# A transformer block in split float32: attention scores in three runs a batch, and one pool of eight PSUM banks

## The reference

```python
def _attention(xq, xkv, wq, wk, wv, wo, bo):
    q, k, v = (xq @ wq), (xkv @ wk), (xkv @ wv)           # each cut into 16 heads of 64
    attn = softmax(einsum('bihd,bjhd->bhij', q, k) * 64 ** -0.5)
    return einsum('bhij,bjhd->bihd', attn, v).reshape(B, S, 1024) @ wo + bo

h = layernorm(x, ln1);   x = _attention(h, h, sa_...) + x        # self attention
h = layernorm(x, ln2);   x = _attention(h, context, ca_...) + x  # context attention
p = layernorm(x, ln3) @ ff_w1 + ff_b1                            # 256 -> 2048
a, gate = p[..., :1024], p[..., 1024:]
return (a * gelu(gate)) @ ff_w2 + ff_b2 + x
```

## Time and profile before

| | |
|---|---|
| median of 3 runs | 2809.46 us |
| profiled execution | 2807.94 us, of which the span (first to last instruction) is 2806.1 us |
| TensorE matmul (PE) | busy 2785.0 us, 99% of the span, 25278 matmuls |
| PE's weight loads (PEld) | 2491.2 us, 89%, beside the matmuls |
| DVE, ACT, POOL | 79%, 67%, 59% |
| granted TensorE clock | 0.999 of full speed |
| chain that ended last | PE 93%, POOL 3%, DVE 2%, all else 2% or less |
| one self batch, one context batch | 35.88 us, 34.07 us |

### The profile page before, as it was taken

How to read it: one execution, slowest core, us unless ns; L and a number is a source line. 1 busy time by engine, 2 the same in 40 slices (tenths; PEclk the granted TensorE clock), 3 DMA queues, 4 the chain that set the end, 5 groups by cost and what they waited for, 6 DMA issues and landing times.

```text
span 2806.1 us, 73115 instructions
## 1 busy us (share of the span) xinstructions
PE 2785.0 (99%) x25278; PEld 2491.2 (89%) x25278; DVE 2215.6 (79%) x3432; ACT 1885.2 (67%) x5979; POOL 1665.0 (59%) x1500
## 2 busy tenths in 40 slices
PE   8999999999999999999999999999999999999999
PEld 7888888888888888888888888888888899999999
DVE  7888888888888888888888888888888855555554
ACT  6777777777777777877777777777777754444443
POOL 5555555555555555776666666666666655544554
PEclk9999999999999999999999999999999999999999
DMA  6666666666666666677777776777677632222222
GB/s 160 150 162 164 164 161 159 159 153 157 154 149 152 153 155 157 152 183 177 181 177 178 180 177 166 170 172 172 166 169 172 153 100 81 75 78 87 77 75 65
DMA packets 355330, 413.34 MB, mean 147 GB/s; under 512 B 122016, under 2 KB 209440, under 8 KB 355232
## 3 DMA queue, kind: packets, MB, share of 16 engines
q1 hardware_dynamic: 345088, 395.29, 58.1%
q10 hardware_dynamic: 10144, 16.78, 1.6%
HBM read 94.52 MB, written 49.02 MB: 51 GB/s over the span
## 4 chain that ended last, share of the span: by engine, by line
PE 93%; POOL 3%; DVE 2%; DMA 1%; issue 1%; ACT 0%; SPq 0%; DVEq 0%; ACTq 0%; POOLq 0%
PE unit_ps L641 53%; PE unit_ps L666 15%; PE s_ps L653 14%; PE s_ps L641 12%; POOL probs L1375 1%; DVE blocks L1141 1%; DVE neg_max L1127 1%; POOL w_lo L1370 1%; ACT probs L926 0%; DVE qk L1153 0%; DMA pT<-blocks 0%; POOL x_rb L1362 0%; DVE w_lo L1087 0%; DVE hT L1122 0%; DMA out_dram<-x_out 0%
## 5 line engine op out<-in xcount | busy, mean ns | idle before, releaser
L1375 POOL TENSOR_TENSOR probs<-probs,row_inv 128x1024 f32<-128x1024 f32 x512 | 971.9, 1898 | 827.0 <-DVE row_inv L1132 827.0
L926 ACT ACTIVATE probs<-s_ps,neg_max 128x256 f32<-128x256 f32 x2048 | 947.0, 483 | 468.4 <-DVE neg_max L1127 467.4
L1141 DVE STREAM_TRANSPOSE blocks<-probs 128x1024 f32<-128x1024 f32 x512 | 633.3, 1237 | 148.4 <-POOL probs L1375 147.8
L1127 DVE TENSOR_REDUCE neg_max<-s_ps 128x4 f32<-128x1024 f32 x512 | 612.9, 1197 | 12.5 <-PE s_ps L653 5.5
L641 PE MATMUL unit_ps<-hT_hi,w_hi 128*128 128x256 f32 x2048 | 579.9, 287 | 4.2 <-DVE hT_lo L1172 2.3
L641 PE MATMUL unit_ps<-hT_hi,w_lo 128*128 128x256 f32 x2048 | 554.7, 277 | 0.0
L641 PE MATMUL unit_ps<-hT_lo,w_hi 128*128 128x256 f32 x1792 | 497.3, 278 | 0.0
L666 PE MATMUL unit_ps<-pT,v_f 128*64 128x256 f32 x4096 | 456.4, 381 | 0.2 <-DMA pT<-blocks 0.2
L653 PEld LDWEIGHTS s_ps<-qk 64*128 64x128 f32 x6144 | 375.3, 185 | 70.5 <-issue 53.4
L926 ACT ACTIVATION_READ_ACCUMULATOR probs<-s_ps,neg_max 128x1 f32 x2048 | 437.5, 214 | 0.0
L653 PE MATMUL s_ps<-qk 64*128 64x256 f32 x6144 | 427.1, 285 | 5.8 <-ACT probs L926 5.3
(11 more groups left out here) (81 smaller groups left out, 4949.0 us busy)
## 6 DMA issues: line engine op xcount, KB each, us to landing
pT<-blocks SPq DMA_DIRECT2D x1024, 256.0 KB, 4.5
rows_t_dram<-row_blocks SPq DMA_DIRECT2D x91, 256.0 KB, 2.3
rows_in<-rows_t_dram SPq DMA_DIRECT2D x91, 256.0 KB, 4.6
x_res<-in_x_dram SPq DMA_DIRECT2D x32, 256.0 KB, 3.1
x_sa_dram<-x_out SPq DMA_DIRECT2D x32, 256.0 KB, 2.2
x_ln<-x_sa_dram ACTq DMA_DIRECT2D x32, 256.0 KB, 4.5
ctx_in<-in_ctx_dram SPq DMA_DIRECT2D x32, 256.0 KB, 4.1
x_res<-x_sa_dram SPq DMA_DIRECT2D x32, 256.0 KB, 3.4
```

The costliest lines, as they stand in the source:

```text
L926: op = nc.scalar.activation(probs[:, m % 2, r, :].rearrange("p (j b c) -> p j b c", j=IT, c=BLK), scored.rearrange("p (j c b) -> p j b c", ...
L1127: nc.vector.tensor_reduce(neg_max[:, m % RING, :], s_ps[:, m % 2, :, :].rearrange("p h (i j) -> p (h i) j", j=S), AX_X, ALU.max, negate=Tr ...
L1141: nc.vector.transpose(blocks[:, n % 2, :, m % 2, :].rearrange("p b (j r c) -> p r j b c", j=IT, c=BLK), probs[:, m % 2, :, :].rearrange("p ...
L1375: nc.gpsimd.tensor_tensor(probs[:, m % 2, :, :], probs[:, m % 2, :, :], row_inv[:, m % RING, :].unsqueeze(2).broadcast_to([P, ROWS, S]), A ...
```

## The change

**Scores in three runs.** TensorE makes pairs 0, 1, 2, then ("qk", 3 to 7) and the second half of an old projection, then pairs 3, 4, then the four attended units, then pairs 5, 6, 7, then queries and keys 0 to 2 of the next batch, the first half of a projection and the values. In context batches the values come first, and keys and projection alternate. The first batch has five runs, the last three. Loops in self attention run over two batches a round, since the place of the rows alternates.

**One pool.** `s_ps` and `unit_ps` become `ps`, eight banks. A table `DOUBLE_OF` gives each pair's scores one of four double banks, `BANK_OF` each other unit one of eight, and `users_before` finds for every bank of a unit who had it last. The ring of split queries and keys has five places.

**Moved work.** Self attention's rows go to two places in turn, and the lo part goes from DVE to POOL. The last attended unit is split like the others by ACT and DVE (POOL's two instructions and `a_last` go). The values in self attention are all copied by ACT; in context attention DVE copies the third of four. `x_rb` goes: POOL adds the bias in place, and the load of `x_res` now waits until the sum has read it, for which it moves to the start of the next batch. In the feed-forward part the residual moves from position 3 to position 6 in POOL's list.

```diff
-K_BEHIND_Q, QK_APART, QK_RING = 368, 640, 2688
+K_BEHIND_Q, QK_APART, QK_RING = 368, 640, 3328
 RING = 4
+SLOTS = 5
-BANKS = 4
+BANKS = 8
...
-STEP_UNITS = (
-    ((("qk", 3), "cur"), (("qk", 4), "cur"), (("qk", 5), "cur"), (("wo", 1), "old")),
...
+RUNS = ((0, 1, 2), (3, 4), (5, 6, 7))
+DOUBLE_OF = (2, 1, 0, 3, 2, 3, 2, 0)
+SLOT_OF = (0, 1, 2, 3, 4, 0, 1, 2)
...
+END_ORDER = (scored(0, 1, 2) + FIRST_GAP + scored(3, 4) + ATTENDED + scored(5, 6, 7) + VALUES[:2] + OUTPUT_FIRST + VALUES[2:])
...
+BANK_OF = {("qk", 3): 6, ("qk", 4): 7, ("qk", 5): 4, ("qk", 6): 5, ("qk", 7): 2, ("wo", 1): 3, ("x",): 3,
+           ("a", 0): 0, ("a", 1): 1, ("a", 2): 2, ("a", 3): 3,
+           ("qk", 0): 2, ("qk", 1): 3, ("qk", 2): 6, ("wo", 0): 7,
+           ("v", 0, 0): 2, ("v", 0, 1): 3, ("v", 1, 0): 6, ("v", 1, 1): 7}
...
-            with eng.Fori(starting + 1, B - 2, 1) as t:
-                iteration(t, STEADY, sa)
+            with eng.Fori(starting + 1, B - 4, 2) as t:
+                for i in range(2):
+                    iteration(t + i if i else t, STEADY, sa, (starting + 1 + i) % 2)
...
             def scores(t, m, to_context=False):
-                pe.wait_ge(at.qk_lo, g + 1)
-                at_least(pe, at.exp_done, g - 1)
+                at.bank_free(pe, t, ("s", m), "cur", to_context)
...
+                for m in RUNS[0]:
+                    scores(t, m, to_context)
+                for m in range(3, PAIRS):
+                    run_unit(t, home, odd, ("qk", m), "cur")
+                if "old" in parts:
+                    run_unit(t, home, odd, ("wo", 1), "old")
...
+                for m in RUNS[1]:
+                    scores(t, m, to_context)
+                for unit, part in ATTENDED:
+                    run_unit(t, home, odd, unit, part)
+                for m in RUNS[2]:
+                    scores(t, m, to_context)
...
             def residual(ph, b, bias):
                 pool.wait_ge(ph.res_ld, 16 * (b + 1))
-                if ph is not ff:
-                    at_least(pool, ph.wo_done, 2 * b - 1)
-                nc.gpsimd.tensor_tensor(x_rb[:], x_res[:], out_bias[:, bias:bias + 1, :].broadcast_to([P, IT, D]),
+                nc.gpsimd.tensor_tensor(x_res[:], x_res[:], out_bias[:, bias:bias + 1, :].broadcast_to([P, IT, D]),
...
-                    if m == 3 and "cur" in parts:
+                    if m == FT - 2 and "cur" in parts:
                         residual(ff, t, 2)
```

More of the change, by code:

```diff
@@ L23 @@
 FF_WHOLE = 2
-STARTING, TURNING = 6, 4
+STARTING, TURNING = 7, 4
 LOADING, FF_LOADING = 12, 12
@@ L76, in by_tensor, with bank_of, banks_of @@
+BANK_OF = {("qk", 3): 6, ("qk", 4): 7, ("qk", 5): 4, ("qk", 6): 5, ("qk", 7): 2, ("wo", 1): 3, ("x",): 3,
[3 rows of a table added]
+LAST_ATTENDED, LAST_OUTPUT = (4, 5, 6, 4), 5
+ROWS_TURNED, TURNED, DOWN = 1, 6, (4, 7)
+def bank_of(unit, b=None):
+    return 0 if unit == ("qk", 2) and isinstance(b, int) and b == 0 else BANK_OF[unit]
+def banks_of(unit, b):
+    return (2 * DOUBLE_OF[unit[1]], 2 * DOUBLE_OF[unit[1]] + 1) if unit[0] == "s" else (bank_of(unit, b),)
 def by_tensor(b):
     return isinstance(b, int) and b < WHOLE
[L81 to L97, removed]
@@ L100, in units_of, with order_of @@
[L100 to L108, removed]
+def order_of(t, to_context, batches):
+    if isinstance(t, int):
+        special = {-1: FILL_ORDER, 0: START_ORDER, batches - 1: END_ORDER}
+        return special[t] if t in special else SELF_ORDER if t + 1 < batches // 2 else CROSS_ORDER
+    return CROSS_ORDER if to_context else SELF_ORDER
@@ new lines, in users_before @@
+def users_before(t, unit, part, batches, to_context):
+    users = []
+    own = batch_of(t, part)
+    for bank in banks_of(unit, own):
+        at, order = t, order_of(t, to_context, batches)
+        place = order.index((unit, part))
+        while True:
+            place -= 1
+            if place < 0:
+                if isinstance(at, int) and at == -1:
+                    break
+                at = at - 1
+                order = order_of(at, to_context, batches)
+                place = len(order) - 1
+            u, of = order[place]
+            b = batch_of(at, of)
+            if bank not in banks_of(u, b) or (isinstance(b, int) and not 0 <= b < batches):
+                continue
+            if u == ("x",) and not by_tensor(b):
+                continue
+            if not any(u == other for other, _ in users):
+                users.append((u, b))
+            break
+    return users
@@ L668, in attend, with projection @@
                 last.then_inc(at.o_full, 1)
-            def projection(slot, cols, side, tokens):
+            def projection(slot, cols, side, context, tokens):
                 terms = []
@@ L728, in run_unit @@
                     cols = slice(c * HALF * P, (c + 1) * HALF * P)
-                    product(bank, [(h, w) for w, h in projection(2, cols, ph.kv, rows)]).then_inc(at.v_full, 1)
+                    side = 1 if ph.has_ctx else own
+                    product(bank, [(h, w) for w, h in projection(2, cols, side, ph.has_ctx, rows)]).then_inc(at.v_full, 1)
                 elif unit[0] == "wo":
@@ new lines, in attention_iteration @@
+                exponentials(t, 0)
+                split_qk(t, 3)
+                exponentials(t, 1)
+                split_qk(t, 4)
+                if pass_of(t, home).has_ctx:
+                    split_qk(t, 5)
+                    split_qk(t, 6)
+                    exponentials(t, 2)
+                else:
+                    exponentials(t, 2)
+                    split_qk(t, 5)
+                    split_qk(t, 6)
+                split_qk(t, 7)
+                if blocks_next(t, parts):
+                    scale_rows(t + 1, home)
@@ new lines, in attention_iteration @@
+                maxima(t, 4)
+                invert_sums(t, 3)
+                if "old" in parts:
+                    project_out(t - 2, 1)
+                attended_lo(t - 1, 0)
+                invert_sums(t, 4)
+                transpose_blocks(t, 3, home)
+                attended_lo(t - 1, 1)
+                attended_lo(t - 1, 2)
+                if not to_context:
+                    attended_lo(t - 1, 3)
+                maxima(t, 5)
+                if to_context:
+                    attended_lo(t - 1, 3)
@@ new lines, in attention_iteration @@
+                if parts == LAST:
+                    deviation(ff, 0)
+                elif norm_ahead(t, parts):
+                    deviation(at, t + 2)
+                normalise(t, 3)
+                normalise(t, 4)
+                residual(at, t - 1, pass_of(t - 1, home).norm)
+                for p in lo_pool(t, 1):
+                    split_piece(p)
+                normalise(t, 5)
+                if to_context:
+                    context_remainders(t + 1)
+                normalise(t, 6)
```

823 lines of the change are left out of this document (481 added, 342 removed), and 7 rows, old and new, of tables (BANK_OF, STEP_UNITS).

## The result

The changed kernel takes 2908.8 us (median of 4 runs, 2907.3 to 2909.9) against 2809.8 (median of 4) for the kernel before; the ratio is 1.035, with an interval of 1.034 to 1.037. The forecast was 2791. Its profiled execution has a span of 2907.8 us, so 101.7 us more than the 2806.1 of before.

What follows compares the result with a forecast made beforehand. The prediction took TensorE's (PE's) instruction stream as the bound. Its terms, -24.2 + 3 + 0 - 3.5 + 4.5 + 0 + 2 = -18.2, took 2807.9 to 2789.7, plus 1.5 to the median: 2791 us, range 2783 to 2802.

Steps and rivals of the forecast that it cites:

- One run of scores fewer: TensorE's stream: 62 batches each lose one isolated run of scores, 0.39 us each, -24.2 us in all.
- Nothing: Bias added in place, later x_res load, ring of five, and a_last's instructions against one more cast and lo part: no cost.
- New waits in context batches: TensorE at ("qk", 7) waits for pair 1's exponentials: 0.1 us per batch, +3 us in 30 batches.
- Self batches: ACT and POOL have room for the moved work and banks come free in time: 0, upper end +9 us.
- own sign of failure: A context batch above 34.1 us would mean DVE's order, not PE, sets it, and the forecast is wrong.
- The slower rival: Pair 7's transposition on DVE waits for POOL, delaying pair 1's exponentials: about 2826 us, lower end 2809, chance 0.08.
- The start: First batch: most waits for exponentials go, part returns as waits on qk_lo: -3.5 us, ends -9 and +2.
- The last batch: Last attention batch: PE waits for x_out behind DVE's split of the feed-forward weight: +4.5 us, ends +1 and +7.
- The feed-forward part: POOL's residual stands later in its list, delaying the last batch's final lo part: +2 us, ends 0 and +4.
- The pass change: Weight splits are spread out, but attended units' lo parts wait for them instead: 0, ends -2 and +2 us.
- The loop of two batches: Self attention's 82 KB loop body may be refetched at some 11 jumps back: 2806 us, no change, chance 0.07.

Runs made afterwards that it cites:

- the mended kernel: Changed kernel with x_out's store behind the moves of pairs 0 to 3, last batch's sum before the weight split, feed-forward residual back at position 3; 2794.0 us.
- keys ahead: The mended kernel with context batches' third key unit ahead of the projection's second half, and ACT's first normalised rows before the first weight split; 2784.9 us.
- the first experiment: The changed kernel with SyncE's store of x_out moved behind the moves of pairs 0 to 3; 2804.8 us.

## Why the prediction was wrong

*One run of scores fewer: right in self batches.* Forecast 0.39 us a batch. With the wait taken away a self batch falls from 35.88 to 35.47, 0.41. A context batch falls by 0.02 in the mended kernel and by 0.28 at best (34.07 to 33.79, keys ahead); the last 0.11 stay open.

*The step that failed* is the one headed "Nothing", and with it "New waits in context batches" and "Self batches". They price banks, maxima, exponentials and sums, and leave out SyncE's queue. What the sum had to count was one wait that the change lengthens, SyncE's for `x_out`, and what is queued behind it: the four moves that free the place, 7.7 us from the first issue to the last landing. The sum `x_out` stood ahead of the maxima of pair 2 before, and stands behind the maxima of pair 4 now, while the transposition that needs the moves now belongs to scores ahead of the attended units.

The margin, in means of self batches 8 to 29 counted from the batch's first scores: before, the blocks land at 20.0 and the transposition starts at 24.3, 4.3 us to spare. With the store behind the moves they land at 23.0, 0.2 us ahead of the transposition: the new order alone uses up the margin. The moves start 2.8 us later, now held by the first attended unit, and the transposition 1.1 us earlier. In the changed kernel the blocks land at 26.2, 3.2 us later again, and DVE waits 3.0 us (2.7 in the stretch shown above): that part is the store. The landing time (4.5 us, the median of all moves) and the rows of SyncE's timeline were in the trace of before and stand in none of the prediction's rows.

The cost of the step: forecast 0 in self and +3 in context batches, measured against the mended kernel 1.80 us in each self and 1.84 in each context batch, and 104 us in all by the first experiment. Some 6.6 us of it are clock: in batches 8, 10 and 59 of the profiled execution TensorE ran a stretch at half its clock, and they take 39.4, 39.4 and 37.7 us where the others take 37.1 (self) and 35.8 (context) in the mean.

The prediction's own sign of failure did appear, a context batch above 34.1 us; it was to mean that DVE's order sets the batch, and DVE was waiting for SyncE.

*The slower rival* had the right form (DVE late in every batch, priced per microsecond and batch) and the wrong link. It blamed pair 7's transposition and POOL's multiplication. In the first experiment POOL's and DVE's lists are untouched and the loss is gone. Its chance of 0.08 was too low for another reason as well: the chances were shared out among the chains that had been worked out, with next to nothing left for all others, and the one that counted went through an engine for which nothing had been worked out.

*Waits in context batches beside that:* forecast 0.1 us, at the key unit of pair 7. Measured in the mended kernel 0.14 there and 0.11 at the scores of pair 2, and the last experiment takes 0.25 off. One of the two places was forecast, and together they cost two and a half times the 0.1. (In that sum the steps of PE add up to 7.54 us, not 7.6, which would have made it 0.16.)

*The start:* forecast -3.5, measured +0.4. The waits for exponentials did go and turned into waits on `qk_lo`, as said. What was not counted is that ACT splits a weight piece ahead of the first rows. ACT's timeline, before and then after:

```profile
6.53 1.43 ACT L903 ACTIVATE x_n<-x_ln,ln_shift,rstd 128x256 f32<-128x256 f32 x2 [3.21 <-POOL ln_shift L1356]
```

```profile
7.27 1.15 ACT L930 ACTIVATE w_hi<-w_stage 128x512 fp32r<-128x512 f32 x2 [3.94 <-DMA w_stage<-in_L_xattn_sa_wk_dram]
8.32 1.43 ACT L959 ACTIVATE x_n<-x_ln,ln_shift,rstd 128x256 f32<-128x256 f32 x2
```

The rows are 1.8 us later because they queue behind a piece that has to be loaded. Putting them first won 0.7 us, not 1.5: TensorE then waits 2.3 us for the lo part of the rows, which stands behind a weight split on DVE. What else takes the forecast gain at the start was not tried apart.

*The last batch:* forecast +4.5 with one wait of 6 to 7 us on `x_out`, measured +8.7 with one of 7.7. The mechanism is right, the size is half of what was measured. The wait itself is 0.9 us over the 6.8 worked out (6.5 in the first experiment, where the blocks are not late). Behind it TensorE ran at a lower clock for some microseconds (below): from the first matmul of the fourth value to the end of the projection half behind it 5.77 us pass in the changed kernel and 4.18 in the mended one, 1.6 us. And of the 2.3 us deducted, 1.5 of them for time lost before, the trace confirms one wait of 1.3 us, behind the third attended unit. That leaves about 0.7 us of the 4.2 which is not explained.

*The feed-forward part:* forecast +2, measured 2.8, with 1.1 to 2.9 between any two profiles of the two orders. *The pass change:* the six batches around it take 211.2 us in the mended kernel and 212.3 before, with six runs of scores saved in it, so about +1.3 beside the saving; forecast 0, with +2 as its upper end.

*The loop of two batches:* no gap of PE in step with it; in the first experiment and in the mended kernel each of the 23 self batches takes 35.47 us to 0.01 us, where PE in the looped part jumps back after every second. The larger body is also fetched once and kept. While the changed kernel loops, from 400 to 1000 us, queue 8 brings no instructions; all that there are:

```profile
q14 instruction: 2, 0.02, 0.0%
```

## What to carry to other kernels

When work is moved forward in one engine's list, follow it to the buffers that it fills, and ask who empties them, in which queue, and what that queue is waiting for at that time. A queue of transfers is an engine in order like the others: write down for each of its waits what is issued behind it, and take issue time (here 8.3 us for eight) and landing (a median of 4.5 us) as steps of the chain. A store belongs behind loads and moves that somebody waits for, unless something waits for the store.

## What was not expected of the hardware

An idle stretch of TensorE can cost more than itself. In the first experiment's last batch (store behind the moves, the weight split still ahead of the sum), windows of 10 us with the wait in the first and second:

```profile
2240.00:2250.00 10.00, 3.56 (x26) 2.99 (x24) 6.01 (x7) 6.27 (x19) 3.49 (x2) 0.94 0.70 164
2250.00:2260.00 10.00, 9.90 (x59) 8.37 (x61) 3.05 (x7) 4.68 (x6) 6.79 (x3) 0.71 0.20 64
2260.00:2270.00 10.00, 10.00 (x90) 8.69 (x86) 4.97 (x11) 4.54 (x7) 5.79 (x3) 1.00 0.58 133
```

The granted clock is 0.94, then 0.71, then 1.00: after PE had stood for 6.5 us, part of the next 10 was run at 1.2 GHz and not 2.4, though PE was busy in 9.9 of them. Batch 8 of the changed kernel shows the same behind a wait of 2.1 us, the low level by itself in the second row:

```profile
331.90:341.90 10.00, 7.96 (x76) 7.63 (x74) 5.94 (x10) 4.78 (x19) 2.24 (x2) 1.00 0.64 176
341.90:345.30 3.40, 3.36 (x8) 2.71 (x9) 3.40 (x5) 2.64 (x11) 1.89 (x1) 0.50 0.47 106
```

A wait of 1.7 us that ends at 532.6 has no such stretch behind it. With the sum made later, where the waits are longer, there are 46 stretches at 0.50 (167 us together), and the granted clock of the whole run is 0.974. The 20 context batches in the loop that hold one take 39.8 us in the mean and the 6 others 39.1; the 12 self batches that hold one take 41.2 and the 11 others 40.3. At 0.8 to 0.9 us each that is some 40 of the 73 us by which this run passed its expectation (an estimate from these means).

A wait off the critical engine comes through in part, and the part grows. DVE's 1.74 and 1.54 us a batch (self, context) cost 0.45 and 0.83 us; its 2.7 and 2.5 us in the change cost 1.80 and 1.84, or 1.59 and 1.77 without the three batches at a lower clock. That the last microsecond of the wait costs more than it is long was not looked into further.
